# Causal attention layer: key tiles in another order, the values' products placed one bank at a time, and queries and keys turned by fp32r products

## The reference, cut to what matters

```python
q = (x @ q_w + q_b) / math.sqrt(HEAD)          # 16 heads of width 8
k = x @ k_w + k_b
v = x @ v_w + v_b
scores = jnp.einsum('bhqd,bhkd->bhqk', q, k)
causal = jnp.tril(jnp.ones((s, s), bool))
scores = jnp.where(causal, scores, neg)
attn = jax.nn.softmax(scores, axis=-1)
ctx = jnp.einsum('bhqk,bhkd->bhqd', attn, v)
```

## Time and profile before

| | us |
|---|---|
| median of three executions | 3524.71 |
| the profiled execution | 3526.23 |
| its span in the trace | 3524.5 |
| causal attention block, first turn to the next block's first product | 648.6 to 855.4, 206.8 |
| PE, DVE, ACT, POOL busy in that stretch | 160.1, 101.9, 88.8, 20.3 |

### The profile page before, as it was taken

One profiled execution on the slowest core, in us unless ns is written; L12 is line 12 of the kernel. 1 busy time (PEld: TensorE's weight loads), 2 busy tenths in 40 slices (PEclk: granted clock), 3 DMA queues, 4 the chain that ended last, 5 costly groups with the idle time before them and its releaser, 6 DMA issues. The chain is left out here.

```text
span 3524.5 us, 50933 instructions
## 1 busy us (share of the span) xinstructions
PE 3180.8 (90%) x18448; PEld 1856.2 (53%) x18448; DVE 2477.8 (70%) x4334; ACT 1689.5 (48%) x2048; POOL 1871.0 (53%) x1159
## 2 busy tenths in 40 slices
PE   5979797586448999999999999999999999999998
PEld 4757576332324555555555555555555555555445
DVE  6979798653258776877777787687777778767533
ACT  5758576243213444444444444444444444444442
POOL 3857575111222655655665565565566556556670
PEclk8989899567679999999999999999999999999998
DMA  1000000000410000000000000000000000000001
GB/s 62 1 1 1 1 1 1 12 1 1 140 22 3 1 1 1 4 1 1 1 4 1 1 4 1 1 4 1 1 1 4 1 1 2 1 1 1 1 1 35
DMA packets 20600, 28.47 MB, mean 8 GB/s; under 512 B 5124, under 2 KB 12424, under 8 KB 20232
## 3 DMA queue, kind: packets, MB, share of 16 engines
q1 hardware_dynamic: 19016, 22.09, 1.9%
q0 software_dynamic: 1344, 3.15, 0.3%
HBM read 21.56 MB, written 3.67 MB: 7 GB/s over the span
## 5 line engine op out<-in xcount | busy, mean ns | idle before, releaser
L2049 ACT ACTIVATE pair_probs<-banks 128x1024 f32<-128x1024 f32 (+1 forms) x944 | 965.5, 1026 | 1035.2 <-PE banks L1959 983.8
L2098 DVE TENSOR_REDUCE pair_peaks<-banks 128x1 f32<-128x512 f32 (+1 forms) x1800 | 1085.6, 665 | 271.4 <-PE banks L1941 257.6
L2191 POOL TENSOR_TENSOR pair_total_pool<-pair_total_pool,pair_probs 128x1536 f32<-128x1536 f32 x208 | 724.6, 3484 | 754.1 <-DVE pair_total L2112 748.9
L1982 PE MATMUL banks<-pair_probs,pair_values 128*64 128x512 f32 (+1 forms) x3776 | 872.8, 600 | 0.0
L1941 PE MATMUL banks<-pair_k_high,pair_q_high 64*128 64x512 f32 (+1 forms) x1920 | 568.0, 443 | 26.6 <-DVE pair_peaks L2091 14.0
L2180 POOL TENSOR_TENSOR pair_total_pool<-pair_total_pool,pair_probs 128x1024 f32<-128x1024 f32 x224 | 535.7, 2392 | 39.1 <-POOL pair_total_pool L2191 21.4
L2112 DVE TENSOR_TENSOR pair_total<-pair_total,pair_probs 128x512 f32<-128x512 f32 (+2 forms) x464 | 457.9, 987 | 94.5 <-ACT pair_probs L2049 69.3
L1982 PEld LDWEIGHTS banks<-pair_probs,pair_values 128*64 128x64 f32 (+1 forms) x3776 | 248.3, 136 | 472.6 <-issue 384.7
L1959 PE MATMUL banks<-pair_q_shift,pair_one_rows 64*128 64x512 f32 (+1 forms) x1888 | 475.4, 396 | 3.1 <-ACT pair_probs L2049 3.1
L1941 PEld LDWEIGHTS banks<-pair_k_high,pair_q_high 64*128 64x128 f32 x1920 | 263.1, 185 | 356.4 <-issue 211.9
L1959 PE MATMUL banks<-pair_q_high,pair_k_high 64*128 64x512 f32 (+1 forms) x1888 | 426.9, 391 | 0.0
(11 more groups left out here) (323 smaller groups left out, 3770.3 us busy)
## 6 DMA issues: line engine op xcount, KB each, us to landing
expert_w<-in_fc SPq DMA_DIRECT2D x32, 256.0 KB, 4.3
context_rows<-in_ctx SPq DMA_DIRECT2D x10, 320.0 KB, 6.4
dense_w<-in_We SPq DMA_DIRECT2D x2, 1024.0 KB, 9.2
experts_in<-expert_zeros SPq DMA_DIRECT2D x1, 1024.0 KB, 3.8
expert_b<-in_fc_b SPq DMA_DIRECT2D x2, 512.0 KB, 4.7
expert_rows<-experts_in SPq DMA_DIRECT2D x16, 64.0 KB, 2.0
experts_out<-expert_result POOLq DMA_DIRECT2D x4, 256.0 KB, 4.6
row_parameters<-in_rows SPq DMA_DIRECT2D x1, 896.0 KB, 8.4
```

The lines of the kernel that those rows point to most:

```text
L1982: last = pe.matmul(out[heads[head], :], values[0:n, ring_of(h // 2, i // 4), i % 4, heads[head]], probs_of(h, i)[0:n, head, :], start=i == ...
L2049: act.activation(probs_of(h, i)[0:n], slot(e)[0:n], ACT.Exp, scale=1.0 / 8.0).then_inc(S["expd"].sem, 1)
L2098: v.reduce_max(peaks[:, head, t, b:b + 1], fill_bank(f, head)[:, 0:width(b)], axis=AX).then_inc(S["peaked"].sem, 1)
L2191: pool.tensor_tensor(pooled[:], pooled[:], three, ALU.add).then_inc(S["pooled"].sem, 1)
```

## The change

1. `causal_order` walks the key tiles in the order 0, 7, 1, 6, 2, 5, 3, 4, so that key tiles with many and with few queries alternate.
2. An add is now one bank of one key tile (4 products instead of up to 8). The adds of the previous key tile are set between the scores of the present one. The ring of `causal_probs` goes by the position in the new order, with its own counts of adds to wait for (`added`).
3. The scores of group g now begin right behind the shift and the last add of group g-1. The turns of queries and keys of group g+1 are set singly behind the first and second score, and the back of g-1 comes behind two more entries of the list than before.
4. The turns of queries, keys and shift are fp32r matmuls with a unit matrix (`causal_ones_by_diagonal`, one more DVE copy of 128x128 at the start) instead of transposes. The back stays a transpose.

```diff
+KEY_TILES = (0, 7, 1, 6, 2, 5, 3, 4)
+def banks_of(j):
+    return range(j // 4, 2)
...
     for g in range(NG):
-        behind = []
-        for j in range(TT):
-            behind += [("score", g) + s for s in scores[j]]
-            if j:
-                behind.append(("add", g, j - 1))
         if g:
-            ahead.insert(min(4, len(ahead)), ("back", g - 1))
-        order += ahead[:2]
-        ahead = ahead[2:]
-        for entry in behind:
-            order.append(entry)
-            if entry[0] == "score" and ahead:
-                order.append(ahead.pop(0))
+            ahead.insert(min(6, len(ahead)), ("back", g - 1))
+        for n, j in enumerate(KEY_TILES):
+            adds = [("add", g, KEY_TILES[n - 1], bank) for bank in banks_of(KEY_TILES[n - 1])] if n else []
+            for m, piece in enumerate(scores[j]):
+                order.append(("score", g) + piece)
+                if ahead:
+                    order.append(ahead.pop(0))
+                while adds and (m + 1) * len(banks_of(KEY_TILES[n - 1])) >= len(scores[j]) * \
+                        (len(banks_of(KEY_TILES[n - 1])) - len(adds) + 1):
+                    order.append(adds.pop(0))
...
+                def turn_parts(unit, rows):
+                    for t in range(TT):
+                        last = pe.matmul(slot(unit)[:, t // 4, t % 4 * P:(t % 4 + 1) * P],
+                                         rows[:, t, group_columns(unit[1]), :].rearrange("p h c -> p (h c)"),
+                                         ones_by_diagonal[:], start=True, stop=True)
+                    last.then_inc(S["made"].sem, 1)
...
-                def add(g, j):
-                    wait(pe, "selected", TT * g + j + 1)
+                def add(g, j, bank):
+                    n = position[j]
+                    wait(pe, "selected", TT * g + n + 1)
                     wait(pe, "taken_scalar", last_score[g, j])
-                    if j == 0:
+                    if n == 0:
                         wait(pe, "kept", g)
-                    for bank in range(j // 4, 2):
-                        a, b = max(j * P, bank * 512), bank * 512 + 512
-                        for h in range(GROUP):
+                    a, b = max(j * P, bank * 512), bank * 512 + 512
+                    for h in range(GROUP):
...
+                    n = TT * g + position[j]
+                    if a == 0 and pair == 0 and n >= 3:
+                        wait(act, "added", added[n - 3])
```

More of the change, by code:

```diff
@@ L924, in causal_order @@
             order.append(("shift", g + 1))
-        order += [("add", g, TT - 1), ("keep", g)]
+        order += [("add", g, KEY_TILES[-1], bank) for bank in banks_of(KEY_TILES[-1])] + [("keep", g)]
     order.append(("back", NG - 1))
@@ L966, in causal_attention @@
         fills_of_group = sum(unit[:2] == ("fill", 0) for unit in units)
+        adds = [unit for unit in order if unit[0] == "add"]
+        added = [max(n + 1 for n, unit in enumerate(adds) if unit[1:3] == (g, j)) for g in range(NG) for j in KEY_TILES]
+        position = {j: n for n, j in enumerate(KEY_TILES)}
         heads = lambda pair: slice(2 * pair, 2 * pair + 2)
@@ L1003, in score @@
                     last.then_inc(S["made"].sem, 1)
-                def add(g, j):
-                    wait(pe, "selected", TT * g + j + 1)
+                def add(g, j, bank):
+                    n = position[j]
+                    wait(pe, "selected", TT * g + n + 1)
                     wait(pe, "taken_scalar", last_score[g, j])
-                    if j == 0:
+                    if n == 0:
                         wait(pe, "kept", g)
-                    for bank in range(j // 4, 2):
-                        a, b = max(j * P, bank * 512), bank * 512 + 512
-                        for h in range(GROUP):
-                            last = pe.matmul(out[PART * h:PART * h + PART, bank, a - bank * 512:512],
-                                             values[:, j, g * GROUP + h, :], probs[:, j % 3, h, a - j * P:b - j * P],
-                                             start=j == 0, stop=j == 4 * bank + 3)
+                    a, b = max(j * P, bank * 512), bank * 512 + 512
+                    for h in range(GROUP):
+                        last = pe.matmul(out[PART * h:PART * h + PART, bank, a - bank * 512:512],
+                                         values[:, j, g * GROUP + h, :], probs[:, n % 3, h, a - j * P:b - j * P],
+                                         start=n == 0, stop=j == [c for c in KEY_TILES if bank in banks_of(c)][-1])
                     last.then_inc(S["added"].sem, 1)
+                wait(pe, "diagonal", 1)
                 for unit in order:
@@ L1037, in _ @@
                         wait(pe, "negated", g + 1)
-                        turn(unit, lambda t: queries_by_row[:, t, group_columns(g), :].bitcast(F32)
-                             .rearrange("p h c -> p (h c)"))
+                        turn_parts(unit, queries_by_row)
                     elif kind == "score":
@@ L1100, in exponential @@
                     wait_made(act, unit)
-                    if a == 0 and pair == 0:
-                        wait(act, "added", TT * g + j - 2)
-                    act.activation(probs[:, j % 3, heads(pair), a:b], slot(unit)[:, :, 0:b - a], ACT.Exp,
+                    n = TT * g + position[j]
+                    if a == 0 and pair == 0 and n >= 3:
+                        wait(act, "added", added[n - 3])
+                    act.activation(probs[:, position[j] % 3, heads(pair), a:b], slot(unit)[:, :, 0:b - a], ACT.Exp,
                                    scale=float(HD0) ** -0.5).then_inc(S["taken_scalar"].sem, 1)
@@ L1114, in _ @@
                     elif kind == "keep":
-                        wait(act, "added", TT * (g + 1))
+                        wait(act, "added", added[TT * g + TT - 1])
                         act.activation(out_sb[:].rearrange("p (b c) -> p b c", b=2), out,
@@ L1121, in _ @@
                 for g in range(NG):
-                    for j in range(TT):
+                    for n, j in enumerate(KEY_TILES):
                         wait(pool, "taken_scalar", first_score[g, j])
-                        diagonal = probs[:, j % 3, :, 0:P]
+                        diagonal = probs[:, n % 3, :, 0:P]
                         pool.affine_select(out=diagonal, in_=diagonal, compare_op=ALU.is_ge, fill=0.0, base=0,
```

10 lines of the change are left out of this document (5 added, 5 removed).

## The result

| | before | after |
|---|---|---|
| median | 3524.71 us | 3542.56 us (3540.73 to 3545.35) |
| ratio, with its 95% interval | | 1.0051 [1.004, 1.0063] |
| profiled execution, its span | 3526.23, 3524.5 | 3542.56, 3540.8 |
| attention block | 206.8 | 226.0 |

The forecast was 3506 with a range to 3522 and "slower" at 0.13. The block is 19.2 us longer. It begins 1.8 us later, and what stands behind it takes 4.7 us less (2664.4 against 2669.1), with the same instructions.

A forecast was written before the change was run, and what follows sets the result against it. Engines working in turns, with DVE idle behind adds, were taken to set the pace. Savings of 0.6 ahead and 5.3, 5.3, 3.5 and 4.0 in the groups made 18.7 us: 3507.5 profiled, 3506 for the median, range 3480 to 3522.

The forecast's parts named there:

- the sum along DVE: A group's time added up along DVE as border, early part and middle: 43.4 us against 48.7 in group 1.
- the early part: Part of a group with the small fills, now with both adds of key tile 0: 8.2 us against 6.89.
- the middle: Rest of a group after the small fills: DVE's work stays 22.40, idle falls to 4.0; 26.4 us against 35.04.
- its own length + 0.4 - 1.1: DVE's idle time behind an add of one bank, in the middle: 5.0 us in all at 1.2 GHz, 0.3 at 2.4.
- With three tenths of the time at the higher clock: PE's clock in the middle, from a mean of 0.65: DVE's idle time behind adds comes to 3.6 us.
- the clock stays down: Rival, chance 0.17: shorter add blocks between scores and fills don't raise PE's clock; 45.9 us a group, 3517 us in all.
- The border: Between groups, from negated peaks to DVE's first read of the next fills: 8.8 us against 6.83 and 7.85, so longer.
- ACT's chain: At the border, after 3.5 us of shift and add: keep, score, queries, score, keys, 5 pieces of 1.0 us, to 8.5.
- the slower rival: Rival, chance 0.13: the fp32r product costs what a plain one does, 4.4 us a turn at 1.2 GHz; 3541 us.
- Edges at nothing: 32 more edges between tilings of adds and scores on PE, taken as free; 11.5 us if each waited out a tail.
- The last group: Group 3, without fills: exponentials 18.4 us with 4 of gaps, last add 1.3; 31.6 us against 35.6, 4.0 saved.
- The first two turns: Start of the block: turns by products save 0.9 us, the unit matrix copy costs about 0.3; 0.6 saved.

The follow-up runs named there:

- the turns in the wait: Kernel before with the turns of the next group's queries and keys moved ahead of the shift, where PE waits for the peaks: 3518.96 us, 0.9987.
- the changed kernel with the filled wait: Changed kernel with twelve transposes of the unit matrix added ahead of each shift, where PE waits for the peaks: 3535.48 us, 1.003.
- the products alone: Kernel before with fp32r products for the turns of queries, keys and shift, and the unit matrix they need, nothing else changed: 3522.44 us, 0.9995.
- spread adds: Changed kernel with the old key tile order and the turns ahead of the first score again, keeping products and one-bank adds between scores: 3534.32 us.

## Why the prediction was wrong

1. *PE left out as a bound.* The failed step is the sum along DVE: the early part and the middle were DVE's work plus its idle time behind adds, at a clock taken as given. The trace had PE busy for 40.3 of 48.7 us at 0.64, and I wrote that off as tails. At 0.50 the middle of group 2 keeps 10.7 us of idle DVE (7.4 in that of group 1), in pieces of at most 1.40 us, each released by PE, where the formula "its own length + 0.4 - 1.1" had 5.0. The middle was 29.1 at a clock of 0.68 and 33.0 at 0.50; predicted were 26.4 as the likeliest and 27.8 at 0.50. The early part was 8.9 and 10.1 for 8.2.
2. *The clock taken over from before.* "With three tenths of the time at the higher clock" was used for a kernel in which the blocks of both banks, behind which it had risen, were to go. I had that very row and used it for a rival only. The adds, all 384 records of them, tell the size (the groups of PE's adds, before and after; busy us, mean ns, idle before):

```profile
L1013 PE MATMUL banks<-causal_probs,values_by_head 128*32 128x512 f32 (+3 forms) x384 | 57.1, 716 | 2.0 <-ACT causal_probs L1103 1.9
```

```profile
L1030 PE MATMUL banks<-causal_probs,values_by_head 128*32 128x512 f32 (+3 forms) x384 | 69.4, 815 | 2.7 <-issue 1.4 <-ACT causal_probs L1120 1.3
```

   12.3 us more for the same products.
3. *The rival "the clock stays down" (0.17) had the right mechanism for the adds*, but its price was off, by the first step: 45.9 us per group and 3517, where the group that ran at 0.50 throughout took 54.0.
4. *The border.* 8.8 was predicted, 10.9 came. A turn by products takes 1.94 us at 1.2 GHz, as by transposes, where I had chosen 1.5. And I added up ACT's chain as if it never waited for PE, whose chain (8.98 from the start of the shift to that of the score behind the keys' turn) is the longer one. The sum that I had made along PE for the slower rival, three turns and 4.29 between them, gives 10.1 with turns of 1.94.
5. *Edges at nothing.* Of the changed kernel at 1.2 GHz, a score and a fill with an add behind them, and the same with a score behind them:

```profile
805.17 0.79 PE L1011 MATMUL banks<-keys,queries 25*128 25x512 f32 x2
805.89 1.94 PE L1030 MATMUL banks<-causal_probs,values_by_head 128*32 128x512 f32 x8
807.76 0.79 PE L1011 MATMUL banks<-keys,queries 25*128 25x512 f32 x2
808.36 0.62 PE L1018 MATMUL banks<-queries,keys 25*128 25x512 f32 x2
```

   The add starts 0.72 us after the fill, the score 0.60; a transpose ahead of a score takes 0.41 in place of 0.24. The 0.73 that I read in the earlier trace rows as no gap was such an edge. So an edge costs 0.12 to 0.17 us at 1.2 GHz, and 32 of them 4 to 5 us, an estimate. The rule of TensorEngine Tiling in the Trainium skill (Key Properties), that changing the mode drains the engine, has the right sign; the 0.36 us that I had worked out for it was too much.
6. *The last group.* 31.6 was predicted, 43.3 came, at 0.58. My sum had 4 us of gaps between the exponentials and 1.3 for the last add. ACT's gaps behind its first exponential come to 14.2, all released by scores (9.5 before, from the back on), and the adds of two key tiles stand behind the last score and take 3.83:

```profile
846.20 0.38 ACT L1120 ACTIVATE causal_probs<-banks 128x256 f32<-128x256 f32 x1 [2.20 <-PE banks L1018]
848.79 3.83 ACT L1120 ACTIVATE causal_probs<-banks 128x1024 f32<-128x1024 f32 x5 [2.20 <-PE banks L1018]
868.93 3.83 PE L1030 MATMUL banks<-causal_probs,values_by_head 128*32 128x512 f32 x16
```

   In the new order a long add meets an exponential of 0.38 us only, so that ACT stands still behind it. The order and the clock were not tried apart here: kernels with the old order took 33.0 to 33.8 us at 0.70 to 0.78, but 38.1 at 0.63 (the turns in the wait), and with the new order the changed kernel with the filled wait took 40.6 at 0.63.
7. *The slower rival (0.13)* had the sign right for a wrong reason: it put the loss on the product's price, and the products alone changed nothing.
8. *The first two turns* gained nothing (28.9 to 29.0 us), where I had 0.6. *Right* was that the long idle times behind adds go: 2.96 and 3.04 us before, at most 2.17 ahead of the read of a fill now. And the middle at about the clock of before (0.68 for 0.65) was off by 2.7 us only.

TensorE: Matmul & The Clock Gate in the Trainium skill (Part 4) says that transposes don't engage the full clock. The runs disagree: twelve transposes in a wait were followed by a turn of 1.11 us in place of 1.94 in group 1 of the changed kernel with the filled wait. They don't show that transposes always do: at two other borders the turn stayed at 1.97, and of 8 traces with transposes for the block's first two turns 2 had no rise behind them.

What stays open: what the clock answers to. A group's clock differs by up to 0.25 between kernels whose groups hold the same work (group 2: 0.75 before, 0.50 with spread adds), and I can't say beforehand at which it will settle. Open too is what the new tile order costs in groups 1 and 2 beyond the clock.

## What to carry to other kernels

Where PE runs at a mean of 0.6 to 0.7 and is busy for 80% of a stretch, as here, add the stretch up along PE at 1.2 GHz as well as along the engine that waits, and take the longer sum. Dealing PE's large blocks out evenly takes idle time from its consumers, but it may take away the dense stretch behind which the clock rose. Work that is due anyway is best put where PE waits: it gained here in both kernels, by 5 and by 13.5 us, of which 4.1 and 9.5 lie in the block.

## What was not expected of the hardware

- Added work that computes nothing made a kernel faster: 3542.6 to 3535.5 us with 48 transposes in the waits, and, less surely, 3574.4 to 3560.3 with more of it.
- Eight fp32r products of 128x128 cost what eight transposes cost, 1.94 to 1.97 us at 1.2 GHz, but in the same place 12 of 12 stretches full of products were followed by 0.50, where 6 of 8 full of transposes were followed by 2.4 GHz (the earlier trace rows has one of them).
- Full-height work set between products of 25 rows took 0.41 us a piece at 1.2 GHz, against 0.24 in a row.
